# GpSimd without the clearing of a spare tile between its indirect DMAs

## The reference

```python
h = relu(layernorm(x)); x = x + gin(h)         # two sums of x[src] by dst, two small MLPs
h = relu(layernorm(x)); x = x + attention(h)   # scores e per edge, softmax over dst, messages
h = relu(layernorm(x)); x = x + tent_conv(h)   # msg = sum_k basis[:, k] * (xj @ w[k]), sum by node
h = relu(layernorm(x)); x = x + spline_net(h)  # below
# spline_net: three times, with K = 125 kernels
z = einsum('ni,kio->nko', x, W).reshape(N * K, Fout)
gathered = z[col[:, None] * K + idx]           # 8 corners of a cell for each edge
msg = einsum('es,eso->eo', basis, gathered)
out = segment_sum(msg, row, N) / max(deg, 1)[:, None] + b
```

## Time and profile before

| what | us |
|---|---|
| median of 3 runs | 11980.05 |
| lowest and highest | 11966.1, 11993.72 |
| span of the profiled execution, first to last instruction | 11729.7 |
| median of the runs less that span | 250.3 |
| TensorE busy | 6194.3 |
| VectorE busy | 6868.2 |
| ScalarE busy | 2989.3 |
| GpSimd busy | 7301.5 |
| the 4944 memsets of the spare tile, busy | 1376.4 |

### The profile page before, as it was taken

One profiled execution on the slowest core, in us unless ns is written; L12 is line 12 of the kernel. 1 busy time (PEld: TensorE's weight loads), 2 busy tenths in 40 slices (PEclk: granted clock), 3 DMA queues, 4 the chain that ended last, 5 costly groups with the idle time before them and its releaser, 6 DMA issues. The chain is left out here.

```text
span 11729.7 us, 173426 instructions
## 1 busy us (share of the span) xinstructions
PE 6194.3 (53%) x40278; PEld 4754.9 (41%) x40279; DVE 6868.2 (59%) x17651; ACT 2989.3 (25%) x7270; POOL 7301.5 (62%) x10729
## 2 busy tenths in 40 slices
PE   4333244444688987666664555555544444662332
PEld 3222244434344443355553555555523333332222
DVE  6555666664322222577787666666656767655555
ACT  0000022221233332111112555555531111220000
POOL 3888788882366665577773333333327877228887
PEclk8555555555688987566665555555565555685555
DMA  6332222224455554222325777777621111587777
GB/s 195 113 113 57 62 62 62 63 62 131 149 190 187 193 186 134 52 74 74 78 77 147 281 285 278 280 284 281 235 81 43 44 41 43 178 323 219 221 222 199
DMA packets 894930, 1760.69 MB, mean 150 GB/s; under 512 B 487010, under 2 KB 487319, under 8 KB 889928
## 3 DMA queue, kind: packets, MB, share of 16 engines
q0 software_dynamic: 317952, 1023.05, 28.3%
q1 hardware_dynamic: 537672, 598.27, 15.2%
q10 hardware_dynamic: 39168, 138.04, 3.0%
HBM read 1150.36 MB, written 611.50 MB: 150 GB/s over the span
## 5 line engine op out<-in xcount | busy, mean ns | idle before, releaser
L1560 POOL DMA_INDIRECT got<-corners,now x1664 | 1679.5, 1009 | 1926.6 <-DVE now L1548 1171.3
L1560 POOL DMA_INDIRECT got<-node_rows,now x1664 | 1639.6, 985 | 1267.3 <-issue 1251.5
L1451 PE MATMUL made_p<-weights,turned 128*128 128x320 bf16 (+4 forms) x7595 | 1541.8, 334 | 203.0 <-ACT z L1417 106.6
L150 POOL MEMSET spare<- 128x192 f32 x4944 | 1376.4, 278 | 3.1
L2342 PE MATMUL sum_p<-msg_s,hot_s 128*128 128x64 f32 x3328 | 734.2, 422 | 931.6 <-DVE msg_s L1824 931.6
L1560 POOL DMA_INDIRECT got<-patches,now x832 | 839.3, 1009 | 565.4 <-DVE now L1548 283.0
L2342 PEld LDWEIGHTS sum_p<-msg_s,hot_s 128*128 128x128 f32 x3328 | 717.7, 332 | 937.5 <-issue 937.5
L1451 PEld LDWEIGHTS made_p<-weights,turned 128*128 128x128 bf16 (+1 forms) x7595 | 657.9, 101 | 1039.0 <-issue 517.0
L896 POOL DMA_INDIRECT d_rows<-row x832 | 942.9, 1133 | 184.3 <-issue 160.1
L1417 ACT COPY z<-made_p 128x384 f32<-128x384 f32 (+3 forms) x1495 | 714.6, 515 | 932.3 <-PE made_p L1451 612.1
L656 POOL DMA_INDIRECT s_rows<-row_now,pos_i x784 | 848.1, 1082 | 155.2 <-issue 136.5
(11 more groups left out here) (411 smaller groups left out, 13596.3 us busy)
## 6 DMA issues: line engine op xcount, KB each, us to landing
corners<-z SPq DMA_DIRECT2D x245, 960.0 KB
corners<-z SPq DMA_DIRECT2D x98, 864.0 KB
d_rows<-empty ACTq DMA_DIRECT2D x32, 1586.0 KB
row<-d_rows SPq DMA_DIRECT2D x104, 488.0 KB
corners<-z SPq DMA_DIRECT2D x49, 672.0 KB
s_rows<-empty ACTq DMA_DIRECT2D x32, 962.0 KB
row<-s_rows SPq DMA_DIRECT2D x104, 296.0 KB
got<-node_rows,now POOLq DMA_INDIRECT x1664
```

Of the source, the lines that this page charges most:

```text
L150: pool.memset(self.of[:, t, :], 0.0).then_inc(self.cleared, 1)
L1451: m = nc.tensor.matmul(self.made_p[s % banks][:, 0:w], self.turned[b][0:rows, stack, :], weight[0:rows, at:at + w], start=n == 0, stop=n = ...
L1560: pool.indirect_dma_start(out=to[b][:, t, :], out_offset=None, in_=table, in_offset=bass.IndirectOffsetOnAxis(ap=indices.now[b][:, t:t + 1 ...
```

## The change

The class `Spare` goes, with its tile, its two semaphores and its three uses: the increment at the start of a phase, the wait at t = 0 and t = 4, and the memset behind each indirect DMA. It is taken out of `place_phase`, `turn_phase`, `second_sum_phase`, `tent_phase`, `spline_phase` and `score_phase`. The indirect DMAs, their order, their `pace` and all other engines stay as they are.

```diff
-class Spare:
-    WIDTH = 192
-    def __init__(self, k, ph):
-        self.of = sb(k, ph, "spare", [LO, T, self.WIDTH])
-        self.cleared, self.seen = ph.sems("cleared", "spared")
-    def begin(self, pool):
-        pool.sem_inc(self.cleared, T)
-    def again(self, pool, g, t):
-        if t % (T // 2) == 0:
-            pool.sem_inc(self.seen, 1)
-            pool.wait_ge(self.cleared, g * T + (t + T // 2))
-            pool.sem_inc(self.seen, 1)
-    def clear(self, pool, t):
-        pool.memset(self.of[:, t, :], 0.0).then_inc(self.cleared, 1)
...
                         for t in range(T):
-                            spare.again(pool, i * 2 + b, t)
                             scattered.pace(pool, i, b, t)
                             pool.indirect_dma_start(
                                 out=s_rows, out_offset=bass.IndirectOffsetOnAxis(ap=pos_i[b][:, t, 0:1], axis=0),
                                 in_=row_now[b][:, t, :], in_offset=None).then_inc(scattered.landing(b, t), 16)
-                            spare.clear(pool, t)
...
-def gather(pool, to, table, indices, i, b, gathered, spare=None):
+def gather(pool, to, table, indices, i, b, gathered):
     for t in range(T):
         gathered.pace(pool, i, b, t)
-        if spare is not None:
-            spare.again(pool, i * len(to) + b, t)
         pool.indirect_dma_start(out=to[b][:, t, :], out_offset=None, in_=table,
                                 in_offset=bass.IndirectOffsetOnAxis(ap=indices.now[b][:, t:t + 1], axis=0)).then_inc(gathered.landing(b, t), 16)
-        if spare is not None:
-            spare.clear(pool, t)
```

More of the change, by code:

```diff
@@ L547, in place_phase @@
         scattered = Landings(ph, "scattered", 2)
-        spare = Spare(k, ph)
         def at(x, b):
@@ L645, in _ @@
             def _(pool):
-                spare.begin(pool)
                 with pool.Fori(0, pairs) as i:
@@ L893, in _ @@
                         for t in range(T):
-                            spare.again(pool, i * 4 + b, t)
                             scattered.pace(pool, i, b, t)
@@ L1587, in _ @@
                         pool.sem_inc(seen, 1)
-                        gather(pool, got, table, indices, i, b, gathered, spare)
+                        gather(pool, got, table, indices, i, b, gathered)
             @block.vector
@@ L1856, in spline_phase @@
         indices = Indices(k, ph, k.spline_i)
-        spare, corners = Spare(k, ph), Corners(C)
+        corners = Corners(C)
         with nc.Block() as block:
@@ L1866, in _ @@
                         pool.sem_inc(seen, 1)
-                        gather(pool, got, conv.table, indices, i, b, gathered, spare)
+                        gather(pool, got, conv.table, indices, i, b, gathered)
             @block.vector
```

## The result

The changed kernel takes 12540.7 us (median of 4 runs, 12532 to 12554) beside 11986.9 us for the kernel before: a ratio of 1.044, with a 95% interval of 1.041 to 1.048. It is slower by 4.4%, where 2.9% faster was forecast.

The account below looks back on a forecast made before the run. GpSimd's list of indirect DMAs was taken to bound placing, turning and spline: -347 + 15 (holds) + 5 (pace) - 20 (other phases) = -347 us, so 11633 us, 2.9% faster; range 11490 to 11790, chance 0.74.

Parts of the forecast that it names:

- The step: Time between successive indirect DMAs without memset: 1.27 us in placing, 1.28 in turning, 1.25 in spline, saving 0.14 to 0.145 each.
- The choice of 0.30 for the scatters: Idle time behind each scatter in placing and turning was taken as 0.30 us, as for the message phase's gathers.
- half of it: Rival: scatters in placing and turning do not shorten as gathers do, 226 us stay away, 11859 us; chance 0.07.
- more than forecast: Rival: the 0.30 us gap belongs to the message phase, so the step falls to 1.12, 685 us saved, 11295 us; chance 0.03.
- The sum of 347 us: Saving where GpSimd is the bound: placing 110, turning 116, spline 121 us.
- The holds: Indirect DMAs stand while VectorE runs two-SBUF-source operations: 282 us in placing, turning and spline, 15 us more charged.
- Slower: Rival: holds in placing, turning and spline met at their very start, 856 us, giving 12207 us; chance 0.10.
- The pace: GpSimd's sequencer waits for the half group eight DMAs back to land; 5 us charged, bounds 0 and 60.
- The other phases: Tent and score phases together gain 20 us, bounds 0 and 60; nothing taken for the second sum.
- Another engine's wait takes the gained time: Last of the conditions listed under which the forecast would be wrong; no size or chance given.
- no gain: Rival: 1.25 us holds only for bursts of eight; an unbroken list stays near today's step, 11980 us; chance 0.06.
- 250 us before and behind the instructions: Difference between the runs' median 11980.05 us and the profiled span 11729.7 us, taken as lying around the instructions and unchanging.

Follow-up runs that it names:

- quick kind: Sessions in which the kernel before takes 10750 to 10757 us.
- slow kind: Sessions in which the kernel before takes 11709 to 11987 us; the changed kernel took 1.0412 to 1.044 of it there.
- the kernel with the tile and the waits kept: Kernel before with only the 4944 memsets removed, a semaphore increment each half group instead: 10342.0 us, 0.9616, and 10345.2 us, 0.9615, in two sessions.
- the one with one column: Kernel before with the memset clearing 1 column instead of 192: 0.9617 and 0.9615 in two sessions, 1.0436 in another.
- the twelve increments: Kernel before with twelve GpSimd semaphore increments replacing each memset: 11512.2 us, 1.0709, in one session and 12388.5 us, 1.0558, in another.

## Why the prediction was wrong, and where it was right

*The step.* 1.27, 1.28 and 1.25 us were forecast and 1.263, 1.289 and 1.25 came, gap 0.305, in both kinds of session. The choice of 0.30 for the scatters, taken from the gathers, was right, and so "half of it" and "more than forecast" fall.

*The sum of 347 us.* In the quick kind it was 144 (placing) + 83 (turning) + 122 (spline) = 349 us for the three phases, forecast 110 + 116 + 121. That the totals agree is luck: two terms were off by 34 and 33 us, in opposite ways. Placing gained more, since its holds fell (time of the scatters above the usual length of one: 91 to 52 us), turning less, since its holds rose (126 to 152). *The holds* as a whole went from 296 to 270 us in these three, against 15 more forecast; in the slow session after changing they were 205, so that *Slower*, by holds, is not what happened. *The pace*: behind the first, the gaps above the usual 0.305 us come to 5.2 us in the spline phase (5 forecast) and 4.5 in placing. *The other phases* gave 61 in tent and 11 in scores, forecast 20 together, bound 60: the term was mis-sized. In the quick kind the tent phase with the clearing is one more in which GpSimd never waits (its gaps exceed the usual ones by 3 us in all; the earlier trace rows showed 145 us of waits, in the slow kind). Without it, 832 steps of 0.139 us less are 116 us, the holds fell by 30 (77 to 48), and 81 us of new waits for VectorE took most of it back. VectorE's small operations there did get quicker by more than I took, which may have kept those waits shorter. One of them in the tent phase, before and after (minimum/median/maximum in ns):

```profile
L692 DVE TENSOR_SCALAR room<-uvw x101: 178/291/382, 8746.9 to 10079.0; 128x24 f32<-128x24 f32 x101
```

```profile
L664 DVE TENSOR_SCALAR room<-uvw x100: 178/179/181, 9108.5 to 10739.3; 128x24 f32<-128x24 f32 x100
```

Sum 349 + 72 = 421, and the kernel as a whole gained 412 to 414. Measured 0.9615, forecast 0.971. All this is the kernel with the tile and the waits kept; the changed kernel itself met no session of the quick kind, and that it would run there as this one does isn't measured; it is concluded from the slow kind, where the one with one column and it are alike.

*The step that failed* is the one that wasn't taken: the chain was followed for GpSimd alone, and the time in which TensorE, VectorE and ScalarE answer one another was taken from the trace as a constant. In the session in which the change was timed it isn't one. With the denser list VectorE got TensorE's results in the spline phase a median of 27 us behind the matmuls that it needed, VectorE stood 683 us before `hot_s` in the spline phase and TensorE 319 in placing, and in the place of the 347 us less that were forecast the time went up by 554. It depends on how densely GpSimd issues, and 1.39 to 1.42 us stood just where placing, turning and spline still lose nothing by it (1192, 1306 and 1236 us, as in the quick kind). "Another engine's wait takes the gained time" stood as the last condition, but had no rival, no price and no chance.

*It could have been seen* in part. The earlier trace rows have 1171 us before the message phase's gathers, 752 us of waits in the second sum and 241 in scores, and I read them as TensorE or VectorE being the bound; but TensorE was busy for 1318 of 1554 us in the second sum, and no engine near the whole of the message phase. The hand-over from TensorE to ScalarE has a median of 1.50 us in the message phase, where the gathers are 1.25 us apart, and 0.04 (90th percentile 0.83) in turning, where the scatters are 1.42 apart: both were in the trace of before. So was the warning in the rival "no gain", which asked whether an unbroken list is bound by something behind it; the answer was yes, by other engines.

*What lies around the span.* I put 250 us before and behind the instructions. In the profiled execution of after it is 1.8 us (12547.4 less 12545.6), and under 3 us in all later ones. The first profile's 11729.7 us and the 11980 us of the runs are two executions' difference, not a cost around them.

## What to carry to other kernels

A filler between GpSimd's indirect DMAs that nobody reads can be a throttle. Before one is removed, compare the time from a producer's end to its consumer's start for each pair of engines, inside and outside the bursts; where it is longer inside, a denser burst can cost the others more than it saves GpSimd. And where the kernel before differs by 10% from session to session, time both kernels in more than one: the sign of a change can differ between them (one column cleared: 0.96 in one kind and 1.04 in the other).

## What the runs showed of the hardware

- The same program takes 10750 to 10757 us in three sessions and 11709 to 11987 us in five. The number of the chip doesn't tell them apart (one number showed both). Undisturbed indirect DMAs take the same in both within 0.5% (0.958 and 0.962 us in placing), and VectorE's busy time in a phase differs little; TensorE's hand-overs don't agree, nor do its matmuls of the second sum, where the granted clock differs (0.302 us at 0.97, 0.328 at 0.87). The kind was the same for all kernels of a session. What makes it is open, the recording of the run included.
- In the slow kind TensorE, in placing, starts an instruction each 0.70 us (a weight load, then its matmul) while indirect DMAs come every 1.26 us: 292 to 403 starts from 164 to 1300 us lie 0.65 to 0.75 us behind the one before, in each of the six slow traces with a mean step of up to 1.33 us, none with the 1.41 of before or the 1.51 of the twelve increments, and none in the quick kind.
- What is late in the slow kind is the change of TensorE's semaphores: 5.2, 2.0 and 1.9 us behind the matmul's end at the place shown of the message phase and 29.5 at that of the spline phase, and there several changes lie within 0.25 us of one another, 1.7 and 4.2 us behind the end of the last gather. The engine that waits starts 0.11 to 0.16 us behind the change. The ends of matmuls are modelled, but in the quick kind 2980 of 2980 changes fit them. In the denser fillers GpSimd's own are late too (188 of 1989 behind the memset of one column).
- The load of the DMA engines doesn't order the losses: they are busy 0.25 of the time in placing and 0.17 in the tent phase, and these phases lost 87 and 304 us, the spline phase at 0.66 lost 92.
- The idle time between two indirect DMAs is 0.305 us. A memset between them starts at once, and the idle time behind it is 0.16 us with 64 or 192 columns and 0.19 with one; a memset of one column (0.12 us) is free.
